# Channel attention: query and key strips through DRAM from batch 3 on, output products in two halves

## The chip, the cores and the metric

The kernel runs on one core of one Trainium2 chip. The metric is the device time of one execution, in microseconds; 0.2% of it is 3.5 us. The engines are TensorE (PE; PEld is its weight load), VectorE (DVE), ScalarE (ACT), GpSimd (POOL) and SyncE (SP, which here only issues DMAs). Each has a queue of its own and they meet at semaphores.

## The reference

Four gated layers run one after the other over `x` of 16 x 128 x 256. Only the first, a cross attention over channels, is touched. Its 128 channels are 16 heads of 8, and the 256 columns are the positions:

```python
q = jnp.einsum('oc,bct->bot', Wq, target) + bq[None, :, None]
k = jnp.einsum('oc,bcs->bos', Wk, source) + bk[None, :, None]
v = jnp.einsum('oc,bcs->bos', Wv, source) + bv[None, :, None]
q = q.reshape(b, HEADS, HEAD_DIM, t)
...
dot = jnp.einsum('bhdt,bhds->bhts', q, k) / math.sqrt(HEAD_DIM)
mask = target_mask[:, :, :, None] * source_mask[:, :, None, :]
dot = mask * dot - (1.0 - mask) * NEG
amap = jax.nn.softmax(dot, axis=-1) * mask
out = jnp.einsum('bhts,bhds->bhdt', amap, v)
```

`target` is the normalised, masked `x` of a batch and `source` its masked context. The result, times a gate, is added to `x`. A ternary feed-forward layer, two token attentions and a layer of experts follow.

## The kernel before

`attend_channels` (L384) does this layer. **A unit** is one head of one batch (256 units, `U` = 16 a batch). Slots `t` run from -16 on over all engines' queues (`SLOTS`); the body of a slot is written out for each engine in one order, and TensorE and ScalarE take two slots at a time (`DOUBLES`). In slot t TensorE makes the first scores of unit t (`first`, L946), the second scores of unit t - 24 (`second`, L963), which are the same scores turned and with the row maximum inside, and behind them the `products` of both slots.

**Strips.** A head has 8 channels, and the scores are wanted to more than one rounded number's accuracy. So each head owns 32 partition rows, a strip: rows 0 to 23 are its 8 channels three times (q: rounded, rounded, rest; k: rounded, rest, rounded), rows 24 to 26 the mask, row 27 the maxima. Four strips stand side by side in the 128 partitions, and `qs` and `ks` hold four such tiles for each of four batches. The weights are laid out so that a projection gives these rows at once: a batch needs four **pieces** (q0, q1, k0, k1), each 128 x 512 in a PSUM bank.

**Building a batch.** While batch b - 1 is in its 16 slots, batch b is built: pieces in slots 0, 4, 8 and 12 (`PIECES`, `project` L912: 2 bias products over 32 rows, `bias` L898, and 6 products of 256 columns in single-pass form), and the values in slots 13 and 15 (`project_v`). ScalarE rounds each piece two slots later (`round_piece`, L804), VectorE puts rounded part and rest together in the strip tile (`stack_piece`, L1102), and the next piece may take the PSUM bank. For batches 0 to 2 (`WHOLE_ROWS` = 3) the bias products are done over all 128 rows. GpSimd has normalised and masked the inputs and split them into rounded part and rest (`normal_x` and `centre_x` in slot 2, `rest_x` and `rest_c` in slot 8, two batches ahead).

**Using it.** VectorE takes the maximum of each unit's first scores (`take_max`, L1111); three PSUM banks (`s1`) serve these. In slot 1 of the next batch the maxima of a batch are turned (`turn_maxima`), ScalarE reads them (`read_maxima`), and SP copies them into row 27 of the strips (`maxima`). The second scores use two banks (`s2`): unit w may start when the exponential of unit w - 2 is done. ScalarE makes the exponential (`exponential`, L838). Four units later TensorE multiplies four heads' exponentials with values and ones (`weigh`, L992: 16 products of 256 columns), always in slots 2, 6, 10 and 14, into one bank `out`, which ScalarE copies in two halves a batch (`copy_out`, L847).

**Closing.** On SP's queue there is per batch, in this order: `gather` (L633: sums and heads to DRAM, heads back), `maxima` of two batches later, `store_inverse`, `spread_inverse` (a broadcast of the inverted sums, L657). VectorE inverts the sums (`invert`, L1118), and GpSimd multiplies, masks and adds to x (`close`, L719). Batch 10 has SP also load 2 MB of weights, batch 12 the next layer's 3 MB. TensorE fills the slots 0 to 23 and 239 to 254 with a weight product (`gram`) for a later layer.

Of the kernel before, what the change touches and what calls it, by code (L numbers as in the profile page):

```python
# [383 lines left out]
def attend_channels(nc, res, io, gate, work, tern):  # L384

    x_sb, ident = res["x"], res["ident"]
    with ExitStack() as stack:
# [22 lines left out]
        qs = s.sb("qs", [P, A_BUFS, A_TILES, DIM], F32R)  # L410
        ks_at = -(-nc.sbuf_base // 32) * 32
        ks = s.sb("ks", [P, A_BUFS, A_TILES, DIM], F32R)
# [25 lines left out]
        add = s.sb("add", [P, DIM])  # L438
        tern.place(tm_at, dead_at, qs_at, ks_at, vt_at)
# [18 lines left out]
        q_stack, k_stack = s.sem("q_stack"), s.sem("k_stack")  # L458
        s1_psum, max_ready = s.sem("s1_psum"), s.sem("max_ready")
# [20 lines left out]
        CLOSING, INVERTED = 35, 9  # L480
# [7 lines left out]
        def built(t):  # L488

            return t // U + 1 if t // U + 1 < BATCHES else None  # L490

# [38 lines left out]
        PIECES = {0: ("q", 0), 4: ("q", 1), 8: ("k", 0), 12: ("k", 1), 13: ("v", 0)}  # L530
# [24 lines left out]
        def bank_of(b, kind, part):  # L555
            return (5 * b + ORDER.index(f"{kind}{part}")) % 2

        def freed(eng, b, kind, part):


            k = 5 * b + ORDER.index(f"{kind}{part}") - 2
            if k < 0:
                return
# [43 lines left out]
        with nc.Block() as block:  # L607

            @block.sync
            def _(sp):  # L610
# [53 lines left out]

                maxima(0)
                maxima(1)
                for b in range(BATCHES):
                    if b == BATCHES - 1:
                        sp.wait_ge(out_psum, A_TILES * 14)
                        tern.send_scale(sp, 0, tern.sT, tern.sraw, tern.FIRST)  # L670
                    gather(b)
                    if b + 2 < BATCHES:
                        maxima(b + 2)
                    if b < BATCHES - 1:
                        store_inverse(b)
                    if b < BATCHES - 1:
                        spread_inverse(b)
                    if b == 10:
                        sp.wait_ge(cm_ready, BATCHES)
                        work.fetch(sp, 1)  # L680
                    if b == 12:
                        sp.wait_ge(v_psum, BATCHES)
                        sp.wait_ge(tgm_ready, 14 - OWN_MASK)
                        tern.load(sp)

            @block.gpsimd
            def _(pool):
# [16 lines left out]
                def rest_x(b):  # L704
                    pool.wait_ge(xm_ready, b + 1)
                    after(pool, q_psum, 2 * (b - 1))
# [37 lines left out]
                rest_c(1)  # L744
                def normal_x(b):
# [4 lines left out]

                for t in SLOTS:
                    b = prepared(t)
                    if b is not None and t % U == 2:
                        normal_x(b)
                        centre_x(b)
                        centre_c(b)
                    if b is not None and t % U == 8:
                        rest_x(b)
                        rest_c(b)
                    if t == REST_POW:  # L760
# [17 lines left out]
            def _(act):  # L778
# [36 lines left out]

                def read_v(b):
# [40 lines left out]
                def before_exponentials(t):  # L857
# [3 lines left out]
                    if built(t) is not None and u in (2, 6, 10, 14):  # L861
                        round_piece(built(t), *PIECES[u - 2])
                    if u == 0 and 0 <= t < ALL:
                        read_v(t // U)
# [32 lines left out]
            def _(pe):  # L897
                def bias(b, kind, part):  # L898

                    freed(pe, b, kind, part)  # L900
                    o = proj[bank_of(b, kind, part)]
                    for j in range(2):
                        if kind == "v":
                            pe.matmul(o[:, j, 0:P], mext[EXT, DIM * b + P * j:DIM * b + P * j + P], bext[EXT, 1024:1152],
                                      start=(j == 0), stop=False, skip_group_check=True)
                        else:
                            c = 512 * (kind == "k") + P * (2 * part + j)
                            pe.matmul(o[:, j, :], bext[EXT, c:c + P], mext[EXT, DIM * b:DIM * b + DIM],
                                      start=(j == 0), stop=False, skip_group_check=True)

                def project(b, kind, part, j):
                    psum_s, k = (q_psum, 0) if kind == "q" else (k_psum, 1)  # L912
                    h, l = ((xh, xl), (ch, cl))[k]
                    if j == 0:
                        if b < WHOLE_ROWS:
                            freed(pe, b, kind, part)
# [8 lines left out]
                    if b < WHOLE_ROWS:  # L925
                        pe.matmul(o, bext[:, w], mext[:, DIM * b:DIM * b + DIM], start=True, stop=False)
                    pe.matmul(o, wh[:, w], h[:, b % 2, :], start=False, stop=False, skip_group_check=b >= WHOLE_ROWS)
                    pe.matmul(o, wh[:, w], l[:, b % 2, :], start=False, stop=False, skip_group_check=b >= WHOLE_ROWS)
                    mm = pe.matmul(o, wl[:, w], h[:, b % 2, :], start=False, stop=True, skip_group_check=b >= WHOLE_ROWS)
# [17 lines left out]
                def first(b, u, t):  # L947
# [44 lines left out]
                def weigh(b, j):  # L992
                    pe.wait_ge(prob_ready, U * b + A_SLOTS * (j + 1))
                    o = out_bank(b, j // 2)
                    if j == 0:
                        pe.wait_ge(v_ready, b + 1)
                    if b == 0 and j == 0:
                        pe.wait_ge(work.gram_lo, work.grams_to(0))
                    if j % 2 == 0 and o is proj[0]:
                        pe.wait_ge(work.gram_lo, work.grams_to(2))  # L1000
                    if j % 2 == 0 and o is not out:
                        pe.wait_ge(k_stack, 2 * BATCHES)
                        pe.wait_ge(v_ready, BATCHES)
                    if j % 2 == 0 and o is out:
                        after(pe, out_copied, 2 * b + j // 2 if b < BATCHES - 1 else 2 * b - 1)
                    for t in range(2):
                        for v in range(A_SLOTS):
                            r = (v + 2) % A_SLOTS
                            mm = pe.matmul(o[A_ROWS * r:A_ROWS * r + A_ROWS, j % 2, :],
                                           vT[:, b % A_BUFS, t, A_TILES * r + j, :],  # L1010
                                           prob[:, (U * b + A_SLOTS * j + v) % PR, t, :], start=(t == 0), stop=(t == 1),
                                           skip_group_check=True)
                    mm.then_inc(out_psum, 1)

                def gram_room(i):
                    if i == 2:
                        pe.wait_ge(k_stack, 2 * BATCHES)
# [4 lines left out]
                def products(t):  # L1022
                    u, b = t % U, built(t)
                    if weighed(t):
                        weigh(*weighed(t))
                    if b is not None:
                        if u in (0, 4, 8, 12):
                            project(b, *PIECES[u], 0)
                            project(b, *PIECES[u], 1)
                        if u in (13, 15):  # L1030
                            project_v(b, (u - 13) // 2)
# [13 lines left out]
                for first_t in DOUBLES:  # L1045
# [8 lines left out]
                    for t in both:  # L1054
                        if built(t) is not None and built(t) >= WHOLE_ROWS and t % U in PIECES:
                            bias(built(t), *PIECES[t % U])
# [7 lines left out]
            def _(dve):  # L1064
# [45 lines left out]

                def take_max(b, u):  # L1111
# [32 lines left out]
                for t in SLOTS:  # L1144
# [3 lines left out]
                    u, b = t % U, built(t)  # L1148
                    if b is not None and u in (2, 6, 10, 14):
                        stack_piece(b, *PIECES[u - 2])  # L1150
# [2794 lines left out]
```

## Time and profile before

| What | Value |
|---|---|
| Median of 3 runs | 1766.65 us (1765.74 to 1768.85) |
| The profiled execution | 1761.46 us, its span 1759.6 us |
| TensorE busy | 1676.9 us (95%), 11824 products |
| VectorE busy | 1139.4 us (65%) |
| ScalarE busy | 992.1 us (56%) |
| GpSimd busy | 584.2 us (33%) |
| DMA | 95.95 MB, 55 GB/s in the mean |

The busy shares are means over the four layers. The layer of the change lies between about 20 and 300 us. A product's record includes its way through the array and, where it is held by a semaphore, some of the wait, so that a busy TensorE is not one at its peak.

### The profile page before, as it was taken

What the parts mean: (1) busy time and instruction counts of PE and PEld (TensorE: products, weight loads), DVE (VectorE), ACT (ScalarE), POOL (GpSimd) and SP (SyncE); (2) the same over time, 40 slices, a digit from 0 to 9 for tenths busy, and PEclk for the clock granted to TensorE, in tenths of its full rate; (3) what the DMA queues carried; (4) which work ended last, traced back from release to release, by engine and by line L of the source; (5) the groups of instructions that cost most, each with busy time, mean ns of one, the idle gap of its engine ahead of it and who ended that gap; (6) DMA issues with size and microseconds to landing.
All of it is one profiled execution on the core that took longest, in us unless ns stands there. A gap on an engine that the chain in (4) does not pass through costs nothing. (4 is left out here: it accounts for less than half of the span.)

```text
span 1759.6 us, 34328 instructions
## 1 busy us (share of the span) xinstructions
PE 1676.9 (95%) x11824; PEld 1419.5 (81%) x11832; DVE 1139.4 (65%) x2540; ACT 992.1 (56%) x2502; POOL 584.2 (33%) x638
## 2 busy tenths in 40 slices
PE   7999997798999999999999999999999998899997
PEld 6666664368788988889898989888898997689985
DVE  6888888897556656656566655555555567954434
ACT  2788875686545555545556555545545543555553
POOL 4444426435511111112122111111111212877774
PEclk9999997899999999999999999999999999999999
DMA  6011122102100100100100011001000004443448
GB/s 209 14 31 32 32 81 96 60 1 101 52 13 13 45 5 14 49 1 13 37 25 25 13 65 37 13 1 37 13 1 13 1 1 122 146 120 118 127 114 291
DMA packets 50371, 95.95 MB, mean 55 GB/s; under 512 B 10838, under 2 KB 30598, under 8 KB 49216
## 3 DMA queue, kind: packets, MB, share of 16 engines
q1 hardware_dynamic: 41619, 71.09, 12.8%
q0 software_dynamic: 7584, 21.37, 4.1%
q8 instruction: 104, 1.70, 0.4%
q10 hardware_dynamic: 1000, 1.26, 0.2%
q14 instruction: 64, 0.52, 0.1%
HBM read 73.85 MB, written 19.25 MB: 53 GB/s over the span
## 5 line engine op out<-in xcount | busy, mean ns | idle before, releaser
L2358 POOL TENSOR_TENSOR hold_wq<-hold_wq,ca_rsum 128x512 f32<-128x512 f32 x128 | 133.9, 1046 | 797.9 <-DVE ca_rsum L2600 797.9
L2218 ACT ACTIVATE hold_wq<-ca_pT 128x512 f32<-128x512 f32 x128 | 76.4, 597 | 381.3 <-PE ca_pT L2425 381.3
L1116 DVE TENSOR_REDUCE a_mx<-a_s 128x2 f32<-128x512 f32 x256 | 164.1, 684 | 37.5 <-PE a_s L959 37.1
L2581 DVE COPY ca_values<-ca_v 128x512 f32<-128x512 f32 x128 | 88.4, 690 | 125.0 <-PE ca_v L2377 124.3
L2375 PE MATMUL ca_qk<-early_x,cw_wqkv_h 128*128 128x512 f32 x384 | 161.0, 419 | 1.3 <-PEq L1577 1.3
L2590 DVE TENSOR_TENSOR hold_wq<-ca_s,hold_wk 128x512 f32<-128x512 f32 x128 | 88.3, 690 | 108.1 <-PE ca_s L2418 105.2
L845 ACT ACTIVATE a_prob<-a_s 128x512 f32<-128x512 f32 x256 | 138.1, 594 | 34.3 <-PE a_s L979 30.8
L2377 PE MATMUL ca_qk<-early_x,cw_wqkv_l 128*128 128x512 f32 x384 | 151.7, 395 | 0.0
L2376 PE MATMUL ca_qk<-early_x,cw_wqkv_h 128*128 128x512 f32 x384 | 151.2, 394 | 0.0
L2498 PE MATMUL ca_acc<-ca_wo_h,ca_oT_l 128*128 128x256 f32 x512 | 145.2, 284 | 0.0
L2497 PE MATMUL ca_acc<-ca_wo_l,ca_oT_h 128*128 128x256 f32 x512 | 145.0, 283 | 0.0
L2496 PE MATMUL ca_acc<-ca_wo_h,ca_oT_h 128*128 128x256 f32 x512 | 145.0, 283 | 0.0
L2418 PE MATMUL ca_s<-ca_qk 128*128 128x128 f32 x1024 | 135.1, 275 | 2.3 <-issue 2.2
L2437 PE MATMUL ca_oT<-hold_wq,ca_values 128*128 128x128 f32 x1024 | 136.3, 277 | 0.2 <-DVE ca_values L2581 0.2
L2211 ACT ACTIVATE hold_wq<-hold_wq,ca_nb,c_rqs 128x128 f32<-128x128 f32 x256 | 122.9, 483 | 11.1 <-DVE ca_nb L2595 10.9
L2418 PEld LDWEIGHTS ca_s<-ca_qk 128*128 128x128 f32 x1024 | 125.2, 191 | 3.6 <-issue 3.4
L2437 PEld LDWEIGHTS ca_oT<-hold_wq,ca_values 128*128 128x128 f32 x1024 | 125.3, 193 | 0.5 <-issue 0.4
L2211 ACT ACTIVATE hold_wq<-hold_wq,ca_nb,ca_evens 128x128 f32<-128x128 f32 x256 | 123.0, 484 | 2.2 <-DVE ca_nb L2595 2.2
L2496 PEld LDWEIGHTS ca_acc<-ca_wo_h,ca_oT_h 128*128 128x128 f32 x512 | 96.7, 189 | 6.2 <-DVE ca_oT_l L2609 0.2
L2497 PEld LDWEIGHTS ca_acc<-ca_wo_l,ca_oT_h 128*128 128x128 f32 x512 | 97.0, 189 | 5.0
L2498 PEld LDWEIGHTS ca_acc<-ca_wo_h,ca_oT_l 128*128 128x128 f32 x512 | 96.9, 189 | 0.0
L2593 DVE TENSOR_REDUCE ca_mx<-hold_wq 128x4 f32<-128x512 f32 x128 | 87.9, 686 | 4.4
(540 smaller groups left out, 4667.2 us busy)
## 6 DMA issues: line engine op xcount, KB each, us to landing
early_big<-slot_results SPq DMA_DIRECT2D x16, 512.0 KB, 7.1
mw_raw<-in_d_expert_w SPq DMA_DIRECT2D x12, 352.0 KB, 5.1
mw_down<-in_d_expert_d SPq DMA_DIRECT2D x1, 2816.0 KB
a_wraw<-a_heads SPq DMA_DIRECT2D x17, 128.0 KB, 2.0
token_rows<-early_rows SPq DMA_DIRECT2D x1, 2176.0 KB, 15.3
hold_wk<-in_c_wkT SPq DMA_DIRECT2D x1, 2064.0 KB
hold_wq<-in_c_wqT SPq DMA_DIRECT2D x1, 2064.0 KB, 8.2
a_heads<-a_osb SPq DMA_DIRECT2D x64, 32.0 KB
```

Of the source, the lines that this page charges most:

```text
L845: act.activation(prob[:, w % PR, :, :], s2_bank(w)[:, :, :], ACT.Exp, scale=1.0 / A_ROOT)\
L1116: dve.tensor_reduce(mx[:, b % 2, :, h], s1_bank(b, u)[:, :, :], AX.X, ALU.max)\
L2211: ins = act.activation(prob[:, p, b, :], prob[:, p, b, :], ACT.Exp, bias=nb[:, p, b:b + 1], scale=row_scale[layer][:, r:r + 1], accum_out= ...
L2358: pool.tensor_tensor(prob[:, k % 2, :, :], prob[:, k % 2, :, :], rsum[:, k % 2, :].unsqueeze(2).broadcast_to([P, GB, TOKENS]), ALU.mult)\
L2375: pe.matmul(out, ah, bh, start=start, stop=False)
L2376: pe.matmul(out, ah, bl, start=False, stop=False)
L2377: return pe.matmul(out, al, bh, start=False, stop=stop)
L2418: mm = pe.matmul(s_ps[:, b, :], qk[:, p, 0, tok], qk[:, p, 1, tok], start=True, stop=True)
L2437: mm = pe.matmul(oT_ps[:, b, :], v[:, g_ % 2, b, c], pT[:, p, b, :], start=True, stop=True)
L2496: pe.matmul(acc[:, b, :], ah, bh, start=(h == 0 and b % 2 == 0), stop=False, skip_group_check=True)
L2497: pe.matmul(acc[:, b, :], ah, bl, start=False, stop=False, skip_group_check=True)
L2498: mm = pe.matmul(acc[:, b, :], al, bh, start=False, stop=(h == 3), skip_group_check=True)
```

## The change

- From batch 3 on q and k of a batch are projected once, in the natural order of their 128 rows, in one joined piece (`join`: 2 bias products over 32 rows and 6 products of 256 columns), with weights picked out of the strip weights by GpSimd (`natural_weights`, six copies in slot 4). The joined piece of batch b stands 24 slots ahead of its first scores, in slot 8 of a period (batch 4's in slot 40, batch 15's in slot 216); batch 3's is in slot 32. ScalarE rounds it (`round_pair`), VectorE makes the rest (`rest_pair`), both two slots later.
- SP sends the rounded part twice and the rest once to a DRAM image of the strips (`send_parts`, three DMAs of 256 KB) and loads the image into `qs` and `ks` by four DMAs (`load_strips`), each for 32 partitions, with 4 KB pieces. Per batch `send_parts` stands ahead of `gather`, and `load_strips` between `store_inverse` and `spread_inverse`. First scores of a batch wait for these loads where they waited for VectorE.
- Mask rows of batches 3 to 15 are made by GpSimd at the start (`mask_rows`, ten operations on 16 partitions) and written to the image by eight DMAs ahead of the first maxima (`send_masks`); zeros follow for batches 3 to 5 and, ahead of batch 1's `send_parts`, for 6 to 15 (`send_zeros`).
- GpSimd prepares a batch's inputs all at once in slot 0; `close` is two slots later.
- The value halves from batch 3 on are in slots 5 and 13, and their PSUM bank is always the second one; ScalarE reads them in slot 14.
- `weigh` is split: 8 products over the first 128 positions in slots 1, 5, 9 and 13, the other 8 in slots 2, 6, 10 and 14, so that every double slot has one half.

```diff
-        CLOSING, INVERTED = 35, 9
+        CLOSING, INVERTED = 37, 11
...
+        def joined(t):
+            b = WHOLE_ROWS if t == U * (WHOLE_ROWS - 1) else (t - JOIN) // U + 2 if (t - JOIN) % U == 0 else -1
+            return b if WHOLE_ROWS <= b < BATCHES and (b > WHOLE_ROWS or t == U * (WHOLE_ROWS - 1)) else None
...
         def weighed(t):
-            w = t - A_LAG - 3
-            if w >= SLOW:
-                w = w - 1 if w >= SLOW + 1 else -1
-            return (w // U, w % U // A_SLOTS) if 0 <= w < ALL and w % A_SLOTS == A_SLOTS - 1 else None
+            halves = []
+            for half in range(2):
+                w = t - A_LAG - (2 + half)
+                if w >= SLOW or w - half >= SLOW:
+                    w = t - A_LAG - 4
+                    if w < SLOW:
+                        continue
+                if 0 <= w < ALL and w % A_SLOTS == A_SLOTS - 1:
+                    halves.append((w // U, w % U // A_SLOTS, half))
+            return halves
...
-        PIECES = {0: ("q", 0), 4: ("q", 1), 8: ("k", 0), 12: ("k", 1), 13: ("v", 0)}
+        PIECES = {0: ("q", 0), 4: ("q", 1), 8: ("k", 0), 12: ("k", 1)}
+        JOIN, VALUES, MASKED, ZEROED = 8, (5, 13), 4, 6
...
+                def send_masks():
+                    sp.wait_ge(mrow_ready, 8)
+                    later = slice(WHOLE_ROWS, BATCHES)
+                    for k in range(2):
+                        for i in range(4):
+                            sp.dma_start(strips[later, 4 * k + 3, A_HEADS * i:A_HEADS * i + A_HEADS, :],
+                                         mrow[k][later, i, :].bitcast(F32).unsqueeze(1)
+                                         .broadcast_to([BATCHES - WHOLE_ROWS, A_HEADS, DIM])).then_inc(mrow_sent, 16)
...
+                def send_parts(b):
+                    p, n = b % 2, b - WHOLE_ROWS + 1
+                    sp.wait_ge(qk_hi, n)
+                    for places in (slice(0, 8, 4), slice(1, 7, 5)):
+                        sp.dma_start(strips[b, places].rearrange("k p n -> p k n"), hi[:, p, :, :].bitcast(F32))\
+                          .then_inc(hi_sent[p], 16)
+                    sp.wait_ge(qk_lo, n)
+                    sp.dma_start(strips[b, 2:6:3].rearrange("k p n -> p k n"), low[:, p, :, :].bitcast(F32))\
+                      .then_inc(lo_sent[p], 16)
+
+                def load_strips(b):
+                    p, i = b % 2, (b - WHOLE_ROWS) // 2
...
+                    sp.wait_ge(hi_sent[p], 32 * (i + 1))
+                    sp.wait_ge(lo_sent[p], 16 * (i + 1))
+                    after(sp, s2_psum, U * (b - A_BUFS + 1))
+                    image = strips[b].rearrange("(k c) (d r j) n -> r (c d) k (j n)", k=2, d=A_HD, r=A_SLOTS)
+                    for r in range(A_SLOTS):
+                        sp.dma_start(qks[A_ROWS * r:A_ROWS * r + A_ROWS, :, b % A_BUFS, :, :]
+                                     .rearrange("p k j n -> p k (j n)").bitcast(F32), image[r]).then_inc(strip_in[p], 16)
+
+                send_masks()
                 maxima(0)
+                send_zeros(WHOLE_ROWS, ZEROED)
                 maxima(1)
+                send_parts(WHOLE_ROWS)
+                load_strips(WHOLE_ROWS)
                 for b in range(BATCHES):
+                    if b == 1:
+                        send_zeros(ZEROED, BATCHES)
+                    if b + 4 < BATCHES:
+                        send_parts(b + 4)
...
                     if b < BATCHES - 1:
                         store_inverse(b)
+                    if b + 4 < BATCHES:
+                        load_strips(b + 4)
                     if b < BATCHES - 1:
                         spread_inverse(b)
...
                 for t in SLOTS:
                     b = prepared(t)
-                    if b is not None and t % U == 2:
+                    if b is not None and t % U == 0:
                         normal_x(b)
                         centre_x(b)
+                        rest_x(b)
                         centre_c(b)
-                    if b is not None and t % U == 8:
-                        rest_x(b)
                         rest_c(b)
...
+                def join(b):
+                    pe.wait_ge(xl_ready, b + 1)
+                    pe.wait_ge(cl_ready, b + 1)
+                    for k, (h, l) in enumerate(((xh, xl), (ch, cl))):
+                        o = proj[0][:, k, :]
+                        pe.matmul(o, whn[:, k, :], h[:, b % 2, :], start=False, stop=False, skip_group_check=True)
+                        pe.matmul(o, whn[:, k, :], l[:, b % 2, :], start=False, stop=False, skip_group_check=True)
+                        mm = pe.matmul(o, wln[:, k, :], h[:, b % 2, :], start=False, stop=True, skip_group_check=True)
+                    mm.then_inc(qk_psum, 1)
...
-                        if u % 8 == 0:
+                        if u % 8 == 0 and b < WHOLE_ROWS:
                             pe.wait_ge(q_stack, 2 * b + u // 8 + 1)
                             pe.wait_ge(k_stack, 2 * b + u // 8 + 1)
+                        if u == 0 and b >= WHOLE_ROWS:
+                            pe.wait_ge(strip_in[b % 2], 64 * ((b - WHOLE_ROWS) // 2 + 1))
```

## Rows read from the trace of the kernel before

**Rows 1.** Windows view: stretch, its length, busy PE, PEld, DVE, ACT, POOL, clock, DMA
```profile
59.19:256.68 197.49, 192.12 (x2213) 129.88 (x2212) 167.35 (x273) 164.62 (x316) 79.84 (x115) 1.00 0.16 40
280.00:284.00 4.00, 0.35 (x2) 0.30 (x2) 4.00 (x2) 0.66 (x2) 3.88 (x3) 0.88 0.11 35
1510.00:1520.00 10.00, 6.70 (x54) 4.94 (x52) 10.00 (x24) 7.81 (x21) 10.00 (x14) 1.00 0.26 73
```

**Rows 2.** Waits view, 60 to 240 us: waiter, releaser, total us, times, longest
```profile
POOL a_add L728 <- DMA a_rden<-a_inverses: 82.3, 11, 8.3
```

**Rows 3.** Groups by shape, 60 to 240 us: count, busy us, mean ns, idle before
```profile
L1116 DVE TENSOR_REDUCE a_mx<-a_s 128x2 f32<-128x512 f32 x192 | 123.0, 683 | 27.2 <-PE a_s L959 27.0
...
L814 ACT ACTIVATE a_hi<-a_proj 128x512 fp32r<-128x512 f32 x48 | 28.4, 592 | 6.4 <-PE a_proj L929 6.4
```

**Rows 4.** Timeline of ScalarE over one period: start, us, operation, idle before it
```profile
155.87 1.08 ACT L845 ACTIVATE a_prob<-a_s 128x512 f32<-128x512 f32 x2
157.56 1.08 ACT L845 ACTIVATE a_prob<-a_s 128x512 f32<-128x512 f32 x2 [0.60 <-PE a_s L979]
158.56 0.60 ACT L814 ACTIVATE a_hi<-a_proj 128x512 fp32r<-128x512 f32 x1
159.19 1.08 ACT L845 ACTIVATE a_prob<-a_s 128x512 f32<-128x512 f32 x2
...
160.88 1.09 ACT L845 ACTIVATE a_prob<-a_s 128x512 f32<-128x512 f32 x2
...
163.29 1.09 ACT L845 ACTIVATE a_prob<-a_s 128x512 f32<-128x512 f32 x2 [0.18 <-PE a_s L979]
...
165.27 1.09 ACT L845 ACTIVATE a_prob<-a_s 128x512 f32<-128x512 f32 x2
...
167.63 1.04 ACT L845 ACTIVATE a_prob<-a_s 128x512 f32<-128x512 f32 x2
...
169.29 1.09 ACT L845 ACTIVATE a_prob<-a_s 128x512 f32<-128x512 f32 x2
...
170.92 0.60 ACT L845 ACTIVATE a_prob<-a_s 128x512 f32<-128x512 f32 x1
```

**Rows 5.** Timeline of TensorE: slot 32, parts of the period of rows 4, slot 240
```profile
59.19 0.39 PE L959 MATMUL a_s<-a_ks,a_qs 32*128 32x256 f32 x2
...
157.24 0.39 PE L908 MATMUL a_proj<-a_mext,a_bext 32*128 32x256 f32 x2
...
158.46 0.38 PE L959 MATMUL a_s<-a_ks,a_qs 32*128 32x256 f32 x2
...
163.12 1.07 PE L1009 MATMUL a_out<-a_prob,a_vT 128*32 128x256 f32 x16
164.12 0.33 PE L941 MATMUL a_proj<-a_wh,a_ch 128*128 128x128 f32 x1
...
164.60 0.39 PE L959 MATMUL a_s<-a_ks,a_qs 32*128 32x256 f32 x2
...
256.68 0.38 PE L959 MATMUL a_s<-a_ks,a_qs 32*128 32x256 f32 x2
```

**Rows 6.** Timelines of GpSimd and of SP's queue, 158 to 173 us
```profile
158.46 0.73 POOL L728 TENSOR_TENSOR a_add<-a_wraw,a_rden 128x256 f32<-128x256 f32 x1 [7.49 <-DMA a_rden<-a_inverses]
...
160.80 1.22 POOL L748 TENSOR_SCALAR a_xn<-x_sb,a_mv,a_rstd 128x256 f32<-128x256 f32 x1
...
165.29 0.73 POOL L717 TENSOR_TENSOR a_cl<-a_cm,a_ch 128x256 fp32r<-128x256 f32 x1
...
169.54 0.34 SPq L655 DMA_DIRECT2D a_inverses<-a_isums  x1
```

**Rows 7.** DMA view, whole span: issues, KB each, median us to landing
```profile
hold_wq<-in_c_wqT SPq DMA_DIRECT2D x1, 2064.0 KB, 8.2
...
cw_raw_vo<-in_c_wo SPq DMA_DIRECT2D x4, 512.0 KB, 3.8
...
a_rden<-a_inverses SPq DMA_DIRECT2D x15, 128.0 KB, 2.4
```

More of the change, by code:

```diff
@@ L562, in freed @@
             if k < 0:
+                return
+            if b >= WHOLE_ROWS:
+                if kind == "v":
+                    eng.wait_ge(k_stack, 2 * WHOLE_ROWS)
+                    eng.wait_ge(v_ready, b)
+                else:
+                    eng.wait_ge(v_ready, WHOLE_ROWS)
+                    after(eng, qk_lo, b - WHOLE_ROWS)
                 return
@@ L860, in before_exponentials @@
                         read_maxima(turned(t - 1))
[L861 to L864, printed above, removed]
+                    if pieces(t) is not None and u in (2, 6, 10, 14):
+                        round_piece(pieces(t), *PIECES[u - 2])
+                    if joined(t - 2) is not None:
+                        round_pair(joined(t - 2))
+                    if values_read(t) is not None:
+                        read_v(values_read(t))
                     if copied(t) is not None:
@@ L990, in turn_maxima, with weigh @@
                     mm.then_inc(mT_psum, 1)
-                def weigh(b, j):
-                    pe.wait_ge(prob_ready, U * b + A_SLOTS * (j + 1))
+                def weigh(b, j, t):
                     o = out_bank(b, j // 2)
[L995 to L1013, printed above, removed]
@@ new lines, in weigh @@
+                    if t == 0:
+                        pe.wait_ge(prob_ready, U * b + A_SLOTS * (j + 1))
+                        if j == 0:
+                            pe.wait_ge(v_ready, b + 1)
+                        if b == 0 and j == 0:
+                            pe.wait_ge(work.gram_lo, work.grams_to(0))
+                        if j % 2 == 0 and o is proj[0]:
+                            pe.wait_ge(work.gram_lo, work.grams_to(2))
+                        if j % 2 == 0 and o is not out:
+                            pe.wait_ge(qk_lo, BATCHES - WHOLE_ROWS)
+                            pe.wait_ge(v_ready, BATCHES)
+                        if j % 2 == 0 and o is out:
+                            after(pe, out_copied, 2 * b + j // 2 if b < BATCHES - 1 else 2 * b - 1)
@@ new lines, in weigh @@
+                    for v in range(A_SLOTS):
+                        r = (v + 2) % A_SLOTS
+                        mm = pe.matmul(o[A_ROWS * r:A_ROWS * r + A_ROWS, j % 2, :],
+                                       vT[:, b % A_BUFS, t, A_TILES * r + j, :],
+                                       prob[:, (U * b + A_SLOTS * j + v) % PR, t, :], start=(t == 0), stop=(t == 1),
+                                       skip_group_check=True)
+                    if t == 1:
+                        mm.then_inc(out_psum, 1)
@@ L1022, in products @@
                 def products(t):
[L1023 to L1031, printed above, removed]
+                    for half in weighed(t):
+                        weigh(*half)
+                    if pieces(t) is not None and t % U in PIECES:
+                        project(pieces(t), *PIECES[t % U], 0)
+                        project(pieces(t), *PIECES[t % U], 1)
+                    if joined(t) is not None:
+                        join(joined(t))
+                    if value_half(t):
+                        project_v(*value_half(t))
                     if turned(t) is not None:
@@ L1054, in _ @@
                     for t in both:
-                        if built(t) is not None and built(t) >= WHOLE_ROWS and t % U in PIECES:
-                            bias(built(t), *PIECES[t % U])
+                        if joined(t) is not None:
+                            join_bias(joined(t))
+                        if value_half(t) and value_half(t)[0] >= WHOLE_ROWS and value_half(t)[1] == 0:
+                            bias_v(value_half(t)[0])
                     for t in both:
@@ L1147, in _ @@
                             take_max(*unit1(n))
-                    u, b = t % U, built(t)
-                    if b is not None and u in (2, 6, 10, 14):
-                        stack_piece(b, *PIECES[u - 2])
+                    if pieces(t) is not None and t % U in (2, 6, 10, 14):
+                        stack_piece(pieces(t), *PIECES[t % U - 2])
+                    if joined(t - 2) is not None:
+                        rest_pair(joined(t - 2))
                     if FIRST <= t - MEASURED + FIRST < BATCHES:
```

124 lines of the change are left out of this document (101 added, 23 removed).

## The prediction

> **What bounds the kernel now.** I read the page's forty slices first: VectorE, ScalarE and TensorE are all busy in the first sixth, which is the channel attention, and the change touches only that. The windows view gives its stretch: slot 32 begins at 59.19 us and slot 240 at 256.68 [rows 5], so the 13 periods in which batches 3 to 15 are projected take 197.49 us, with TensorE busy for 192.12, VectorE 167.35 and ScalarE 164.62 [rows 1]. A busy share of 97% names TensorE, but the order of events names two limits. The timeline of ScalarE is the view to read: each double slot has one pair of exponentials, and the distance from one pair to the next is the double slot's time. In one period the pairs start at 155.87, 157.56, 159.19, 160.88, 163.29, 165.27, 167.63, 169.29 and 170.92 [rows 4]: steps of 1.69, 1.63, 1.69, 2.41, 1.98, 2.36, 1.66 and 1.63, together 15.05.
>
> Five of the eight steps are 1.63 to 1.69. That is a **loop**, and no engine is full in it: the second scores of a double slot may start only when the exponentials two units back are done, so a step is the pair (1.08) plus what it takes to get scores for the next pair. The pair at 157.56 shows it: ScalarE sat idle 0.60 before it, waiting for the scores [rows 4]. An operation of 0.6 on ScalarE fits into that gap: 158.56 holds a rounding, and the step is still 1.63. Only the other three steps are TensorE's: the one with the last key piece and half of the values (2.41), the one with 16 output products and the other half of the values (1.98), and the one with a query piece and the turned maxima (2.36).
>
> **Part by part.**
> *Projection.* Per batch it loses four pieces (8 bias products and 24 of 256 columns) and gets one joined one (2 and 6), the size of one old piece. An old piece costs TensorE from 157.24, the bias, to 158.46, the next scores: 1.22 us [rows 5]. Three times that, 3.7 us a period, leaves TensorE, but most was hidden by the loop. What is gained is only the three long steps' excess over 1.66, the mean of the five: 0.75 + 0.32 + 0.70 = 1.77 us.
> *Output products in halves.* 16 products take from 163.12 to 164.12, 1.00 us [rows 5]. A half is no less than 0.50; it enters and leaves its mode once more, for which I take 0.05. Each double slot now has 0.55 instead of 0 or 1.00. In the slots with nothing else the loop hides it.
> *The joined slot (slot 8 of 16).* It has bias, join and a half: 1.22 + 0.55 = 1.77. The old piece alone made a step of 1.63 (157.56 to 159.19), with 158.46 as the start of the next scores [rows 4, 5]; 0.55 later gives 2.18 if ScalarE's rounding still stands right before that pair (158.56 and 0.60 long [rows 4]), and a little less if, with the join now ahead of the half, it is done by then. I take 2.1, 0.45 over the loop.
> *Values.* Their halves go to slots 5 and 13, each beside a half of the output products. From 164.12 to 164.60 a value half takes 0.48 [rows 5]; with 0.55, and 0.35 for the bias in slot 5, it is 1.0 to 1.4 of products, where the old piece had 1.22 and still stepped 1.63. Cost nothing; 0.1 if the cover is short.
> *ScalarE and VectorE.* Three roundings of 592 ns [rows 3] and three subtractions go per batch; they were in the loop's gap, so the gain is nothing. VectorE's two maxima are 2 x 0.683 = 1.37 per step of 1.66 [rows 3], so it has room for the one 128x512 subtraction.
>
> **Sum.** An ordinary period: 7 x 1.66 + 2.1 = 13.7. Slots 32 to 223 are twelve of these, and the first has two joins: 12 x 13.7 + 0.45 = 164.9. The last period has none: 8 x 1.66 + 0.2 = 13.5. Together 178.4 against 197.49: 19 us less.
>
> **What is added: the DRAM round trip.** SP issues per batch two stores of 256 KB, one more of 256 KB, and four loads of 256 KB, 1 MB in all, each into 32 partitions. The trace has no such load. Bounds: 2064 KB land in 8.2 us and 512 KB in 3.8 [rows 7], so 1 MB streams in about 2.8 us at that slope; the other end, four times that (11 us), is what a quarter of the partitions could at worst mean. I take 3 to 6. The Trainium skill, SBUF — State Buffer, section "Door 1: The DMA port swizzle", speaks against the change here: 32 partitions reach half of the ports, measured there at 189 GB/s, which would be an estimate of 5.5 us for this megabyte; no run here shows it yet.
>
> The loads stand on SP ahead of the broadcast of the inverses, and that one holds GpSimd. With the first scores of a period as zero (164.60 [rows 5]), the inverses are stored at 169.54, which is +4.9 [rows 6]; the shorter first step and the missing subtraction on VectorE make it about +4.2. The loads follow from +4.5 and stream D us; the broadcast lands 2.4 [rows 7] behind them. Then GpSimd closes a batch (158.46 to 160.80, 2.3 us) and prepares the next (160.80 to 166.02, 5.2) [rows 6], and now the join needs that preparation by slot 8, about +7.2 of the next period. So a period is at least 4.5 + D + 2.4 + 7.5 - 7.2 = 7.2 + D, and by the scores that read the strips at the next zero, with 1.5 for the landing, 6 + D. At D = 2.8 that is 10, at 5.5 it is 12.7: both below 13.7, **hidden**. GpSimd now waits 82.3 us in 11 times for that broadcast [rows 2], so it has the time, but the margin is 1 us at D = 5.5.
>
> **One-offs.** Mask rows and zeros are 1.7 MB and 1.6 MB of 1 KB rows from few partitions, issued by SP ahead of the maxima of batch 0 and ahead of the stores and sums of batch 1. The inverse on VectorE waits for those sums, and for the sums of batch 11 behind the 2064 KB load of 8.2 us [rows 7]. Each may hold VectorE by 0 to 5 us; I take 1.5 for each. Strips of the first joined batch are due 13.7 us after their join, with stores and loads one after the other; I take 0.5. GpSimd's new rows at the start (ten operations on 16 partitions, six copies of weights) fall in its idle time before slot 21. Together 3.5, bounds 0 to 11.
>
> So 19 - 3.5 = 15.5 us. The profiled execution is 1761.46 (span 1759.6 and 1.9 around it), 5.2 under the median of 1766.65; I carry the same distance over: **1751**. From slot 240 on nothing is removed (TensorE's gram and the weights of the next stage move with the slots), so the gain is kept.
>
> **Rivals.**
> *The round trip is not hidden* (the slower side): the chain above sets the period as soon as 7.2 + D passes 13.7, that is D over 6.5; at D = 7.85 it is 15.05 and everything is lost; at D = 9, twelve periods of 16.2 against 15.05 are 14 us longer; with 3.5 of one-offs and the last period 2.8 shorter that is 14.5 us slower, 1781. For it: each load fills 32 partitions only, and SP's stores share the queue. Against it: DMA engines are busy for 0.16 of the stretch [rows 1]. Chance 0.13, of which 0.03 still leaves a gain.
> *The loop is tighter than I read it.* Three score banks serve two maxima and one turned block in a period; if VectorE's pair (1.37 plus hand-over) then sets the steps, a period is 14.8 and the gain 197.49 - 13 x 14.8 = 5 less 3.5: 1765. For it: VectorE is 0.85 busy [rows 1]. Against it: its own work falls. Chance 0.10.
> *TensorE loses its clock.* It now idles some 0.6 in each step. From 280 to 284 it was busy 0.35 of 4 and the granted clock fell to 0.88 on its way to a half; but from 1510 to 1520 it was busy 6.70 of 10 and kept 1.00 [rows 1], and the new stretch is denser. At half the clock its products, at most 11.4 us a period (15.05 less 3.7), take up to 22.8; at 18 a period is 3 longer than now: 36 us slower, 1803. Chance 0.03.
> *It doesn't do what it says*: the gain is there but one-offs of 10 us and a period of 14.3 eat it down to 1765. Chance 0.06.
>
> **Numbers.** The forecast has 0.68. Its own range: periods of 13.4 to 14.2 and one-offs of 0 to 8, that is 22 less to 6 less, 1744 to 1761. To leave out no more than 2 in 10 it reaches to 1765. Faster by over 0.2% (3.5 us, about what a measurement of this kernel can tell from no change): 0.68 + 0.03 and part of the doubtful cases, 0.74. Within: 0.12. Slower: 0.14.
>
> **What will show it.** Steps of 1.63 to 1.69 between exponential pairs in seven of eight double slots and one of about 2.1; TensorE waiting for exponentials, not the reverse; a period near 13.7. If the period is long and TensorE waits for GpSimd's rests or for the strips, the round trip was mis-sized; if VectorE waits for the sums at batches 1 and 11, the one-offs were. If the long step is missing, the half beside the join was hidden.

## The result, and the profile after

| | before | after |
|---|---|---|
| Median of the runs | 1766.20 us (4 runs, 1764.63 to 1768.85) | 1781.20 us (4 runs, 1773.01 to 1783.75) |
| Ratio | | 1.008, 95% interval 1.0056 to 1.0105 |
| The profiled execution, its span | 1761.46 us, 1759.6 | 1773.01 us, 1771.1 |
| Mean granted clock of it | 0.984 | 0.971 |

The change was forecast to take 15.5 us off and put 15 on. The profiled execution of after is the fastest of its four, 8 us under their median, so that the account below covers 11.5 of the 15 us. The windows view of after (columns as in [rows 1]): its first line answers the first of [rows 1], from slot 32 to slot 240; the second and third are two pieces of it, around slots 64 to 80 and slots 224 to 240.

```profile
61.98:269.14 207.16, 185.35 (x1901) 101.21 (x1901) 144.51 (x235) 143.30 (x278) 80.38 (x115) 0.91 0.65 160
...
97.80:128.50 30.70, 16.57 (x127) 8.27 (x127) 10.76 (x18) 9.38 (x18) 6.46 (x10) 0.50 0.55 119
...
252.40:272.00 19.60, 17.66 (x147) 8.67 (x144) 11.11 (x19) 11.27 (x23) 2.18 (x3) 0.74 0.54 139
```

The 13 periods take 207.16 instead of 197.49 us, while TensorE is busy for 6.8 us less and VectorE for 23 less. The granted clock, 1.00 throughout in before, is 0.91: from 97.8 to 128.5 it was at the lower of its two levels.

Where they went is read period by period, from one product of turned maxima (TensorE, out a_s, in ident and a_mx) to the next. These are differences of start times in the timeline, in us:

| Slots | before | after | difference |
|---|---|---|---|
| 16 to 32 | 14.96 | 18.94 | +4.0 |
| 32 to 64, two periods | 15.23, 15.06 | 13.96, 13.99 | -2.3 |
| 64 to 80 | 15.05 | 33.68 | +18.6 |
| 80 to 224, nine periods | 15.04 to 15.32 | 13.98 to 14.10 | -9.7 |
| 224 to 240 | 15.46 | 19.61 | +4.2 |
| 240 to 256 | 16.3 | 16.53 | +0.2 |
| ahead of slot 16, behind slot 256 | | | -0.4, -3.0 |

They add up, within 0.1, to the 11.5 us between the two spans. Eleven periods gained a little over 1 us each, as the change meant; three periods lost 27.

**An ordinary period** on ScalarE answers [rows 4] (start, us, operation, idle before it):

```profile
160.64 1.09 ACT L986 ACTIVATE a_prob<-a_s 128x512 f32<-128x512 f32 x2 [0.61 <-PE a_s L1134]
161.66 0.60 ACT L955 ACTIVATE a_hi<-a_proj 128x512 fp32r<-128x512 f32 x1
162.73 1.08 ACT L986 ACTIVATE a_prob<-a_s 128x512 f32<-128x512 f32 x2 [0.47 <-PE a_s L1134]
...
164.42 1.08 ACT L986 ACTIVATE a_prob<-a_s 128x512 f32<-128x512 f32 x2
...
166.10 1.08 ACT L986 ACTIVATE a_prob<-a_s 128x512 f32<-128x512 f32 x2
167.79 1.08 ACT L986 ACTIVATE a_prob<-a_s 128x512 f32<-128x512 f32 x2 [0.61 <-PE a_s L1134]
...
169.57 1.09 ACT L986 ACTIVATE a_prob<-a_s 128x512 f32<-128x512 f32 x2 [0.46 <-PE a_s L1134]
```

The joined slot steps 2.09 (160.64 to 162.73), the slot of the turned maxima 1.78 (167.79 to 169.57), the others 1.68 to 1.70, those with a half of the values among them. The three long steps of [rows 4] are gone. TensorE's timeline tells which slot is which: halves of the values (out a_proj) at 165.02 and 171.87, the turned maxima at 168.24.

```profile
165.02 0.33 PE L1094 MATMUL a_proj<-a_wh,a_ch 128*128 128x128 f32 x1
...
168.24 0.39 PE L1144 MATMUL a_s<-ident,a_mx 128*16 128x128 f32 x2
...
171.87 0.33 PE L1094 MATMUL a_proj<-a_wh,a_ch 128*128 128x128 f32 x1
```

In the joined slot TensorE ends the join, does a half of the output products, and only then the next scores:

```profile
160.32 0.39 PE L1053 MATMUL a_proj<-a_mext,a_bextn 32*128 32x256 f32 x2
...
161.56 0.64 PE L1164 MATMUL a_out<-a_prob,a_vT 128*32 128x256 f32 x8
162.12 0.38 PE L1114 MATMUL a_s<-a_qks 32*128 32x256 f32 x2
```

From 160.32 to 162.12 is 1.80, against the 1.22 of an old piece [rows 5]; the half is 0.56 of it (161.56 to 162.12).

**The period of slots 64 to 80.** The waits view from 20 to 340 us, then the queue of SP, VectorE and TensorE in time:

```profile
POOL a_add L831 <- DMA a_rden<-a_inverses: 116.6, 13, 24.5
...
PE a_s L1114 <- DVE a_mx L1283: 17.0, 4, 14.8
DVE a_isums L1291 <- DMA a_sums<-a_osb: 16.9, 2, 15.9
```

```profile
84.16 1.03 SPq L725 DMA_DIRECT2D a_strips<-a_mext  x2
86.52 10.48 SPq L734 DMA_DIRECT2D a_strips<-a_hi  x2
97.04 4.31 SPq L737 DMA_DIRECT2D a_strips<-a_low  x1
101.39 3.77 SPq L653 DMA_DIRECT2D a_sums<-a_osb  x1
105.21 4.72 SPq L649 DMA_DIRECT2D a_heads<-a_osb  x4
```

```profile
110.84 0.35 DVE L1291 RECIPROCAL a_isums<-a_sums 128x32 f32<-128x32 f32 x1 [15.87 <-DMA a_sums<-a_osb]
```

```profile
111.80 0.57 PE L1114 MATMUL a_s<-a_qks 32*128 32x256 f32 x1 [14.84 <-DVE a_mx L1283]
```

The two zero transfers (640 KB each, batches 6 to 15) are issued in 1 us, but the next two stores, usually 0.90 us of issue, take 10.48, and batch 1's sums go out at 101.39. VectorE stands 15.87 us before their inversion, the maxima behind it on its queue, and so TensorE stands 14.84. The granted clock falls to a half at 97.8, during the stall, and stays there to 128.5, 16.7 us behind its end. The page's DMA rates, for 84 to 108 us in 40 slices of 0.6; to about 88 us these are the strip loads issued from 81.73 on:

```profile
GB/s 218 191 218 239 212 178 222 268 142 90 97 79 70 73 68 169 138 73 67 73 75 85 116 198 44 49 44 48 48 72 236 53 49 44 49 44 50 41 60 158
```

From 89.4 to 97.2 most slices are at 67 to 97, from 98.4 to 106.8 most at 41 to 53; the higher ones between hold other packets too.

**The period of slots 224 to 240** is the same in small: the 2064 KB of weights stand ahead of batch 11's stores and sums, the maxima that SP sends behind those come late, TensorE waits for them and the granted clock is at a half from 261.6 to 271.8. SP's queue, and TensorE:

```profile
244.06 0.58 SPq L128 DMA_DIRECT2D hold_wq<-in_c_wqT  x1
246.40 0.90 SPq L734 DMA_DIRECT2D a_strips<-a_hi  x2
...
257.64 0.35 SPq L697 DMA_DIRECT2D a_wraw<-a_heads  x1
258.04 0.57 SPq L680 DMA_DIRECT2D a_qks<-a_mT  x1
```

```profile
260.05 0.39 PE L1134 MATMUL a_s<-a_qks 32*128 32x256 f32 x2 [1.62 <-DMA a_qks<-a_mT]
```

In the period before, the same maxima were issued at 239.71, 18.3 earlier; before had them 15.67 apart there (243.02 and 258.69).

### The profile page after: what moved, and what is told of

Read it like the earlier page. It is cut to its first block and busy times, and to the rows that moved or that the text cites. A ratio compares the mean times of both kernels' runs of the same rounds, so it can differ in the third digit from the quotient of the medians.

```text
span 1771.1 us, 33713 instructions
## 1 busy us (share of the span) xinstructions
PE 1671.6 (94%) x11512; PEld 1390.4 (79%) x11520; DVE 1115.9 (63%) x2501; ACT 969.2 (55%) x2463; POOL 590.7 (33%) x654
## 3 DMA queue, kind: packets, MB, share of 16 engines
q1 hardware_dynamic: 59845, 98.36, 19.4%
## 5 line engine op out<-in xcount | busy, mean ns | idle before, releaser
L1114 PE MATMUL a_s<-a_qks 32*128 32x256 f32 x512 | 97.3, 366 | 17.8 <-DVE a_mx L1283 17.0
L1114 PEld LDWEIGHTS a_s<-a_qks 32*128 32x128 f32 x512 | 55.4, 191 | 63.8 <-DVE a_mx L1283 33.1
```

The lines of the kernel that those rows point to most:

```text
L1114: mm = pe.matmul(s1_bank(b, u)[:, t, :], qs[rows, b % A_BUFS, j, P * t:P * t + P], ks[rows, b % A_BUFS, j, :], start=True, stop=True)
```

## The experiments

Two theories stood against each other. **A:** three bundles of one-off transfers (mask rows, zeros, weights) are too slow or badly placed; they stall VectorE and TensorE, and the half clock after each stall adds to it. **B:** the denser loop itself costs the clock or collides with the strips' traffic, whatever the bundles do.

**Zeros from as many partitions, elsewhere.** The second bundle read mext in partitions 6 to 15; here it reads ten partitions six apart from 64 on.

```diff
-                                     mext[a:b, 0:DIM].bitcast(F32)...
+                        rows = mext[a:b, 0:DIM] if a < ZEROED else mext[64:64 + 6 * (b - a):6, 0:DIM]
```

> One edit to the changed kernel: the ten rows of zeros that are written 64 times each come from partitions 64, 70, ... 118 instead of 6 to 15. Sizes, number of rows (1280 of 1 KB) and the ten-way outer size stay. Theory A, the place of the source sets the rate: VectorE's wait of 15.9 us for the sums of batch 1 falls under 4 us and the period of 33.7 us to 14 to 18. Rival B, ten engines with 128 small rows each, or 64 reads of one partition, set the rate: the wait stays at 14 to 17 us.

Measured 1772.01 us, one execution. The same bytes from the same number of partitions moved faster, and the wait for batch 1's sums fell from 15.87 to 6.46. DMA rates from 84 to 100 us (to about 88 us strip loads again), then SP and VectorE:

```profile
GB/s 277 205 195 184 246 236 195 225 200 161 215 146 223 246 236 243 241 228 220 261 310 187 179 195 189 190 166 289 220 54 46 46 56 79 287 248 95 112 88 77
```

```profile
86.64 7.55 SPq L735 DMA_DIRECT2D a_strips<-a_hi  x2
```

```profile
101.57 0.35 DVE L1292 RECIPROCAL a_isums<-a_sums 128x32 f32<-128x32 f32 x1 [6.46 <-DMA a_sums<-a_osb]
```

So where the source lies set most of the bundle's rate: rival B, a wait of 14 to 17, is out. Theory A's own figures (under 4, a period of 14 to 18) were missed. The period is 24.53 instead of 33.68, but the clock now stayed at a half to 138.6 and the next period was 19.17, which gave half of the gain back.

**Zeros from 64 partitions, each row once.**

> One edit to the changed kernel: the zeros of batches 3 to 15 are read from 64 partitions (64 to 127), each row once, instead of from 3 and 10 partitions 64 times. Bytes and place on SP's queue stay. Theory A: the wait for the sums of batch 1 goes, the period of 33.7 us becomes 14.0 to 15, and with the half clock behind it some 19 us leave the span: about 1752 against 1771.1. Rival B, the 1.3 MB ahead of the stores in one queue are themselves too much: 4 us of the wait stay or more, the span falls by 10 at most.

Measured 1767.22 us, ratio 1.0012 (0.9983 to 1.0041), above what theory A gave. The two transfers land 7.9 us after their issue, the stores behind them 7.6 after theirs instead of 14.7, and VectorE's wait is down to 0.68, not the 4 of rival B:

```profile
a_strips<-a_mext SPq DMA_DIRECT2D x2, 640.0 KB, 7.9
a_strips<-a_hi SPq DMA_DIRECT2D x2, 256.0 KB, 7.6
```

```profile
98.60 0.35 DVE L1291 RECIPROCAL a_isums<-a_sums 128x32 f32<-128x32 f32 x1 [0.68 <-DMA a_sums<-a_osb]
```

The period is 16.84: SP still stood 2.35 at the store of the rests (93.34), TensorE waited 1.42 for the maxima, and the granted clock was at a half from 102.7 to 106.1. The edit turns the order of the rows as well as their place, and no run parts the two. More was lost in the other two periods: 20.07 in slots 16 to 32, 20.16 in 224 to 240. The ten executions went from 1753.34 to 1777.25 us with mean granted clocks from 0.983 to 0.959; a straight line through them has 0.52 us more for each us of clock missing. The 23 of before beside them (1759.91 to 1769.66) kept 0.978 to 0.984. At equal clock, 0.98, the lines give 1756 and 1766. That fits a gain that the clock took back, but it does not show it: the clock falls behind stalls, and the lines do not part the two.

**The weights a batch later; and wide zeros, weights later, masks on both sides of the first maxima together.**

```diff
-                    if b == 10:
+                    if b == 11:
```

> One edit to the changed kernel: the load of 2 MB of weights for the gram is issued one batch later on SP's queue (behind the broadcast of batch 11 instead of batch 10), so that the stores of the last joined batch and the sums of batch 11 no longer stand behind it. Theory A: TensorE's wait of 1.6 us for the maxima at 258 to 260 and the half clock from 261.6 to 271.8 go, and the period of 19.6 us becomes 14.5 to 16, if the weights land in time for slot 239. Rival C, that period is long because the gram and the last value half stand there: it stays above 18.

> Three edits to the changed kernel: zeros from 64 partitions, the 2 MB of weights one batch later, and four of the eight mask DMAs behind the first maxima instead of ahead of them. If the three held-up places (19 us at batch 1, 4 to 5 at batch 11, 3 to 4 at the start) are all that keeps the change from its gain of 1.05 us a period, the span is about 1744 and the time some 15 us under the kernel before. If something else gives the gain back, it is 1755 to 1765.

Measured 1783.79 for the first alone (one execution), 1761.98 (ratio 0.9998, 0.9978 to 1.0017) for all three together, inside the range that stood for "something else". Part of that else is the edit itself. The later fetch was a mistake: the gram needs those weights, and where the 1.6 us wait was there is now one of 5.41 on TensorE, 5.33 with all three, and periods of 21.4 and 21.3. In the second kernel:

```profile
251.88 1.20 PE L151 MATMUL a_proj<-hold_wq 128*128 128x258 f32 x2 [5.33 <-DMA hold_wq<-in_c_wqT]
```

**Output products unsplit**, the last kernel's three edits kept:

```diff
-                w = t - A_LAG - (2 + half)
...
+                w = t - A_LAG - 3
+                if w >= SLOW:
+                    w = w - 1 if w >= SLOW + 1 else -1
```

> The last run's kernel (wide zeros, masks around the first maxima, weights a batch later) with the output products unsplit, 16 of them in every second double slot as before the change. By the prediction's reading of the loop a step hides 1.22 us of products, so 16 products alone (1.00) are hidden and the joined slot falls from 2.08 to 1.65: ordinary periods of 13.4, 0.6 shorter than with halves, 7 us less in the whole: 1755. Rival (16 products don't fit beside the scores: steps of about 1.98 in four slots, as the one of them in the kernel before): periods of 14.6 to 14.9, 7 to 10 us more: 1770.

Measured 1754.61, ratio 0.993 (0.9909 to 0.9951). Ordinary periods are 13.45 against 14.00. ScalarE over one:

```profile
156.10 1.09 ACT L985 ACTIVATE a_prob<-a_s 128x512 f32<-128x512 f32 x2 [0.61 <-PE a_s L1133]
157.12 0.60 ACT L954 ACTIVATE a_hi<-a_proj 128x512 fp32r<-128x512 f32 x1
157.74 1.09 ACT L985 ACTIVATE a_prob<-a_s 128x512 f32<-128x512 f32 x2
...
159.43 1.09 ACT L985 ACTIVATE a_prob<-a_s 128x512 f32<-128x512 f32 x2
...
161.06 1.09 ACT L985 ACTIVATE a_prob<-a_s 128x512 f32<-128x512 f32 x2 [0.19 <-PE a_s L1133]
162.75 1.08 ACT L985 ACTIVATE a_prob<-a_s 128x512 f32<-128x512 f32 x2 [0.61 <-PE a_s L1133]
```

The joined slot steps 1.64 (156.10 to 157.74), and the slots with all 16 products 1.63 to 1.69. The second half of the change thus costs 0.55 a period here: the loop hides 1.0 us of products whole, and splitting them only lays a half into the one slot that was full. That the whole came so near to 1755 is partly luck: in the profiled execution slots 64 to 96 took 17.62 and 17.56, behind a wait of 1.17 for the maxima and with the granted clock at a half from 97.5 to 118.0. The period of slots 16 to 32, still built in pieces, is 15.1 unsplit and 16.1 split at full clock (next runs).

**Bundles taken apart.** Mask rows and four zero rows a batch go to DRAM once, and each batch's rows are then copied from there into the image, inside DRAM; the weights come in quarters of four heads.

```diff
+                def fill(b):
+                    for k in range(2):
+                        sp.dma_start(strips[b, 4 * k + 3].rearrange("(i h) n -> i h n", h=A_HEADS),
+                                     mdram[k, b - WHOLE_ROWS].unsqueeze(1).broadcast_to([8, A_HEADS, DIM]))\
+                          .then_inc(zeros_sent, 16)
...
+                    if b + 5 < BATCHES:
+                        fill(b + 5)
+                    if 7 <= b <= 10:
+                        sp.wait_ge(cm_ready, 4 * (b - 6))
+                        work.fetch(sp, 1, b - 7)
```

Both, then each alone:

> All bulk copies are taken apart: the mask rows and four zero rows a batch are stored to DRAM once (four small stores), each batch's mask and zero rows are then copied inside DRAM by two transfers of 128 KB one batch ahead, and the 2064 KB of weights come in four quarters, one a batch. Theory (the lost 30 us were one-off copies from few partitions in SP's queue, and the half clock after the stalls that they made): periods 1, 4, 14 and 15 fall to about 14.0, 14.4, 15.0 and 16.4 us, ordinary ones stay 14.0; the marks from the first to the last turned maxima are 215 us apart (before 228.0, after 242.9); the whole is 12 to 14 us under the kernel before, some 1750 against 1764. Rival 1 (TensorE loses clock in the denser stretch whatever is copied): 1757 to 1763. Rival 2 (two more transfers a batch make the round trip too long): ordinary periods of 14.5 or more, 1758 or more.

> As the first of these four, but the 2064 KB of weights stay in one piece behind batch 10. Theory: period 4 falls from 33.7 to about 14.4 and period 1 from 18.9 to 14, period 14 stays at 19.6 or so with a granted clock of a half for some 10 us in it; about 1755. Rival (the end is long for another reason than these weights): period 14 the same as in the first of these four.

> The changed kernel with nothing but the weights taken in four quarters, one a batch from batch 7 on. Theory: period 14 falls from 19.6 to 15 and the half clock from 261 to 272 us goes; period 4 stays at 33.7; 4 to 5 us less than the changed kernel, about 1776. Rival (batch 11's sums are late through its own strips, not the weights): no change, 1781.

| Periods, us | 16 to 32 | 64 to 80 | 224 to 240 | 240 to 256 | time |
|---|---|---|---|---|---|
| after | 18.94 | 33.68 | 19.61 | 16.53 | 1781.20 |
| both | 16.10 | 14.00 | 19.31 | 17.61 | 1752.31, ratio 0.992 (0.9901 to 0.9938) |
| inside DRAM only | 16.09 | 14.00 | 21.59 | 16.79 | 1755.74, one execution |
| quarters only | 20.54 | 33.68 | 14.20 | 16.52 | 1774.74, one execution |

Each edit takes away its own loss and leaves the other: theory A, for the first two bundles together and for the weights. Ordinary periods stay at 14.00 with a granted clock of 1.00, which speaks against theory B. One miss: with both, slots 224 to 240 stayed at 19.31. There batch 10 issues a copy inside DRAM and a quarter of the weights in one, the maxima of batch 13 go out at 235.61, and a small wait was followed by a granted clock of a half from 238.5 to 252.1:

```profile
237.67 0.38 PE L1134 MATMUL a_s<-a_qks 32*128 32x256 f32 x2 [1.52 <-DMA a_qks<-a_mT]
```

**Unsplit products too, and the copies inside DRAM one batch earlier.**

> The kernel with copies inside DRAM and weights in quarters, its output products unsplit (16 in every second double slot), and each batch's copy inside DRAM one batch earlier, so that batch 10 issues the last quarter of the weights alone. Theory: unsplit products make period 1 15.1 (with halves 16.1) and ordinary periods 13.45 (with halves 14.0); batch 11's maxima come in time, TensorE does not wait 1.5 us there, keeps its clock, and period 14 is 13.7 to 14.3 instead of 19.3. From the first to the last mark 207 us (221.5 with both), the whole some 1739. Rival (the wait and the half clock in period 14 come from the strips of the last batches and not from what batch 10 issues beside them): period 14 stays at 18 or more, 1744.

Measured 1746.54, ratio 0.9903 (0.9879 to 0.9926): faster than both kernels, by 18 and 35 us. Slots 224 to 240 take 14.56; as two edits were made at once, it is not shown which of them did it. From the first to the last product of turned maxima it is 210.1, not 207: the four periods with a quarter of the weights are 14.1 to 14.8. In one of them TensorE waited 0.73 for strips (195.88) and the clock was at a half from 197.8 to 201.2, so there the room in the round trip was used up.

**The round trip, priced.** A copy of 768 KB inside DRAM that nobody reads, ahead of each batch's strip loads.

> As the other kernel of this pair, but ahead of each batch's four strip loads SP issues a copy of 768 KB inside DRAM that nobody reads, so that the loads land later. It prices the round trip. Theory (a period is at least about 7 us plus the time D from the loads to the end of their landing): with D from 4.9 to some 8 or 9 the broadcast of the inverses comes 3 to 4 us later, GpSimd's rests miss the joined slot, and ordinary periods are 15 to 16.5 us instead of 13.45: 20 to 35 us more. Rival (the round trip has much more room than the prediction's 1 us): ordinary periods stay within 0.3 us of 13.45.

Measured 1789.35, one execution. The periods from slot 64 to 224 are 14.0 to 19.4. The last strips now come after the scores that read them, and a period behind such a wait runs at a half clock:

```profile
114.37 0.58 PE L1116 MATMUL a_s<-a_qks 32*128 32x256 f32 x2 [1.52 <-DMA a_qks<-a_strips]
```

```profile
115.10:134.50 19.40, 19.13 (x150) 10.96 (x146) 11.17 (x18) 11.09 (x21) 10.24 (x15) 0.50 0.69 196
152.20:166.20 14.00, 12.58 (x147) 7.66 (x146) 11.08 (x18) 10.92 (x21) 4.19 (x8) 1.00 0.71 185
```

1.9 us more of landing (6.5 instead of 4.6 in the median of a load), and the loads issued some 0.6 later behind the copy, gave a wait of 1.52. That leaves about 1 us of room in periods of 13.45, a rough figure from one wait, in line with the 1 us worked out for 13.7. But the scores that read the strips came to wait, not the join behind GpSimd's rests, which the prediction had as the tighter of the two.

## Why the prediction was wrong

**What held.** The loop of exponential pairs was read rightly: the three long steps went, the joined slot stepped 2.09 where 2.1 was forecast, the loop 1.69. A half cost TensorE 0.56 (0.55 taken), the values nothing, as taken. The round trip was hidden, so that its rival's 1781 meets the measured time by chance: its mechanism was not there. SP issued the loads at 227.56 and GpSimd had the broadcast behind them at 235.26; less 2.4 for that broadcast [rows 7] the loads took about 5.3, inside the 3 to 6 taken. The Trainium skill, SBUF — State Buffer, section "Door 1: The DMA port swizzle", had given an estimate of 5.5 there, and the trace agrees.

**A term a little small.** An ordinary period was to be 13.7 and is 14.0. Two costs showed: 1.69 for a step instead of 1.66, and 0.1 for the turned maxima, which the sum had at nothing when it took off the whole excess of their long step (2.36), though they stay. That is 3.7 us of the 28.8 between 178.4 forecast and 207.16 measured, when the two long periods below are taken off. Left out altogether were slots 16 to 32, where halves stand beside old pieces: 16.1 against 14.96 of before and 15.1 unsplit, so 1.1 us.

**The step that failed is the one-offs.** The text named all three places, and for two of them what waits there, and then took 3.5 us with bounds of 0 to 11. Its own sign of being wrong came true: VectorE waits for the sums, 15.87 at batch 1 and 1.04 at batch 11. Against a period of 14.0, the one of slots 64 to 80 lost 19.7 us, that of 224 to 240 lost 5.4 (to the 14.2 with quarters), that of 16 to 32 lost 2.8 (to the 16.1 without mask rows and zeros from few partitions; the granted clock was at a half from 56.8 to 60.2), 27.9 in all. Three things were left out of that term:

- *The rate.* "0 to 5 us each" had no row behind it. The rows of before show wide transfers only [rows 7]. The zeros of batches 6 to 15 are 1.3 MB from ten partitions (the prediction's 1.6 MB are all of the zeros, really 1.7, and 0.4 of them go earlier), and moved at 67 to 97 GB/s in most slices to 97 us and at 41 to 53 in most of those behind. The ten partitions of the first experiment ran at about 200. The section of the Trainium skill that the prediction cited for the destination, "Door 1: The DMA port swizzle" in SBUF — State Buffer, tells the two sources apart as well: partitions 6 to 15 reach three of its ports, by its 27 GB/s each an estimate of 82, and those of the first experiment reach eight. The trace agrees to 97 us; behind that two ports, an estimate of 54, would fit, as the third has only two of the ten partitions, but no run shows which were left.
- *The queue.* SP did not run ahead of the slow transfer without limit: it stood 10.48, 4.31, 3.77 and 4.72 us at the next issues, so the sums did not only land late, they were sent 12 us late. At batch 11 the longer wait was not VectorE's 1.04 but TensorE's 1.62 for the maxima that SP sends behind the sums, a path that the text did not have.
- *The clock.* The rival "TensorE loses its clock" was put to the ordinary slots, where the clock stayed at 1.00 (0.99 over 126.1 to 252.4). It fell where TensorE had stood still: to a half for 30.7 us in and behind the long stall, and for 10.2 behind one of 1.62. In slots 64 to 80 some 15.5 us are the wait itself and the other 4 the slower products behind it.

Of the rivals, that of the one-offs had the mechanism but stopped at 10 us and 1765, which is also the range's upper end.

**What stays open.** The part behind slot 256 is 3.0 us shorter in after though nothing in it changed, and differs between kernels by several us; its half-clock stretches lie elsewhere in each trace. That the room in slots 16 to 32 is spent by halves beside old pieces is shown by 15.1 against 16.1, but no run split them from slot 32 on only. No run takes away the mask rows alone either, and none was profiled at the median of after, so that the last 8 us between 1773.01 and 1781.20 are not followed to a place; the mean granted clock was 0.971 in the first and 0.961 to 0.964 in the other three.

## What to carry to other kernels

Price a one-off transfer like a loop's: bytes over a rate measured for partitions like its own, at the source as well as at the destination, and then list every transfer queued behind it and who waits for those. A stall of TensorE cost more than its length here, as the products behind it ran at the lower clock: spread bulk over the loop's free DMA time, or copy inside DRAM from rows stored once. And where a loop hides a block of work whole, splitting it gains nothing and may fill the one slot that is full.

## What the runs showed that was not expected

- Ten source partitions at 41 to 97 GB/s in most slices and ten others at about 200, the same bytes and the same packets.
- Issues on SP of 3.8 to 10.5 us behind a slow bundle, where the same instructions usually issue in 0.4 to 1.6.
- Short waits of TensorE followed by long stretches at half of the granted clock, without a fixed relation: 0.73 and 1.42 us by 3.4, 1.52 by 13.6, 1.62 by 10.2. One of 5.33 went with 6.9, and the stalls of 5.4 to 14.9 us in slots 64 to 80 (the changed kernel, zeros from elsewhere, weights later, quarters only) went with 30.7 to 47.8 us of it.
- Copies of 128 KB inside DRAM, one source row to 16 places, stayed hidden beside a loop that already moved 160 GB/s (ordinary periods 14.00 with and without).
